# The first loads in another order, and six blocks of 384 tokens in place of nine of 256 ahead of the experts

## The chip, the cores and the metric

The kernel runs on one core of one Trainium2 chip. The metric is the device time of one execution in microseconds (us), the median of several runs. Times inside an execution come from a hardware trace of one profiled execution.

## The reference

The input is 2 sequences of 2048 tokens with 256 values each, 4096 tokens in all. A diagonal state layer with a residual is followed by a mixture of experts; each is followed by a layer norm.

```python
decays = sigmoid(x @ Wd + bd);  inj = x @ Wi + bi
h[t] = decays[t] * h[t-1] + inj[t]                  # a scan along the tokens
y = layernorm(x + layernorm(h) * gamma + beta + x)
gate = y @ Wg.T + routing_bias                      # 8 experts, the 4 best of each token
weights = softmax over the 4 best
ffn(u, w1, w2, w3) = (silu(u @ w1.T) * (u @ w2.T)) @ w3.T        # hidden size 682
out = layernorm(y + ffn(y, shared) + sum_e weights[e] * ffn(y, expert e))
```

## The kernel before

**First stage.** The tokens pass in eight steps (`NSTEP`) of 512, and the two sequences take turns. For step s, TensorE makes the products with Wd and Wi (`products`), ScalarE the decays and injections (`acts`), VectorE scans (`scan`), TensorE turns the states (`states`), VectorE takes the first norm and adds the residual u (`first_norm`), GpSimd works out the reciprocal deviations (`rstd1`, `rstd2`), ScalarE writes y (`normed`), TensorE turns y (`y_turned`) and makes the gate logits (`gates`). TensorE runs two steps ahead with the products.

**First loads.** SyncE issues, in this order: one half of the weights Wd and Wi (L479), the second half of the turned input of step 0, the other weights, the small parameters, the turned input of step 1, `load_residual(0)` (the rows of x for step 0, L485), `load_turned(2)` (the turned input of step 2, which waits for the products of step 0, because it goes to the same buffer), `load_residual(1)`. GpSimd adds half of beta to each residual (`add_beta`, L594) and fetches the shared weights into `stage` (`fetch(0)`, 2176 KB) between `add_beta(0)` and `add_beta(1)` (L624 to L626); its next work is `rstd1(0)`. ScalarE splits the staged weights in step order (`shared_high`), VectorE makes the low halves (`shared_low`).

**Blocks.** All feed-forward work goes in blocks of tokens against one weight set. Values and weights are held as two float16 parts, so a product is three matmuls. `up` makes six chunks of the hidden layer (66 matmuls as wide as the block), ScalarE takes the silu of each chunk, VectorE multiplies (`gated`), ScalarE rounds (`high`), VectorE makes the rest (`low`), and `down` takes the chunks back to 256 values. A block of `TB` = 256 tokens keeps a chunk in one bank of psA, so four chunks are in flight. A block of `TL` = 384 tokens needs two banks for a chunk, so two chunks are in flight (`chunk_bank`, L287), and its third group of down sums lies in bank 3 of psA, so that chunk 1 of the next block waits until these sums are read (`down_read`). An expert whose count of 128-row groups is odd ends on such a block.

**Order of blocks.** The shared expert runs over all 4096 tokens in 16 blocks of 256: `S1` = 9 ahead of the experts, seven behind them. Pieces of block 0's `up` fill TensorE's waits in steps 6 and 7 (`EARLY`). In the nine blocks, VectorE also does the routing: `chosen_early`, `chosen_late` (the four best of each token), `count`, `places` (the row in the experts' buffer for each token and choice), `weigh`, `pads`, `sizes`, and the low halves of y (`low_half`), and the low halves of expert 0's weights (`first_low`), of which ScalarE makes the high ones (`first_high`). VectorE runs strictly in the order of the code: one such step stands between two chunks' products, or between two blocks (L1520 to L1542).

**Rows for the experts.** When `places` and `weigh` are done, GpSimd scatters the rows of y to memory, 32 indirect DMAs for each of the four choices (`scatter_first` L675, then `scatter`), with expert weights converted beside them. SyncE loads the rows of an expert's blocks turned (L511) with their routing weights (L517) once the scatter for that choice has landed. At the end GpSimd gathers the experts' results back.

## Time and profile before

| | |
|---|---|
| median of 3 runs | 1010.56 us (1007.47 to 1012.38) |
| the profiled execution | 1012.52 us, of which the trace's span is 1010.8 us |
| TensorE (PE) busy | 982.8 us, 97% of the span |
| VectorE (DVE), ScalarE (ACT), GpSimd (POOL) busy | 56%, 51%, 54% |
| chain that ended last, by engine | PE 81%, DVE 6%, POOL 5%, issue 3%, ACT 2%, DMA 2% |

PE is TensorE's matmuls and PEld its weight loads; SPq, ACTq and POOLq are the queues' own instructions. L12 is line 12 of the kernel. In a timeline or a chain a row begins with its start and its length in us; what stands in square brackets is the idle time of the engine before it and what ended that. "x66" is the count of instructions merged into a row. Matmuls overlap, so a row's length is up to 0.17 us more than its share of time.

### The profile page before, as it was taken

The numbers are of one execution on the slowest core, as the hardware profiler recorded it, in microseconds if no ns is written. First come the engines' busy times: TensorE is split into PE (matmuls) and PEld (weight loads), VectorE is DVE, ScalarE is ACT, GpSimd is POOL, SyncE is SP. The second block draws the span as 40 slices with busy tenths as digits, with TensorE's granted clock in tenths as the row PEclk, the third lists the DMA queues.
The fourth block names the chain that finished last, engine by engine and source line by source line (L and its number), as shares of the span: only waits on it lengthen the run. The fifth ranks groups of instructions, "written<-read, shape, count | busy, mean of one in ns | idle before, by whom it ended". The sixth has DMA issues, their size and how long they took to land.

```text
span 1010.8 us, 25795 instructions
## 1 busy us (share of the span) xinstructions
PE 982.8 (97%) x8252; PEld 817.2 (81%) x8252; DVE 570.9 (56%) x1450; ACT 515.7 (51%) x1289; POOL 544.1 (54%) x513
## 2 busy tenths in 40 slices
PE   8999989999999999999999999999999999999987
PEld 3566878878887888888788878788888887887865
DVE  4899887756454555545445445445455454544776
ACT  3666634544454545545455445445455554544466
POOL 3554057669333377237471007066888880875882
PEclk9999999999999999999999999999999999999999
DMA  6766133453533333532514213317973882895694
GB/s 244 198 159 148 47 91 119 108 176 95 166 93 96 94 98 95 163 101 67 143 51 136 63 32 101 93 48 171 126 111 69 123 129 52 112 128 94 94 165 110
DMA packets 168052, 113.88 MB, mean 113 GB/s; under 512 B 113596, under 2 KB 160191, under 8 KB 166848
## 3 DMA queue, kind: packets, MB, share of 16 engines
q0 software_dynamic: 29808, 58.37, 27.1%
q1 hardware_dynamic: 115888, 33.15, 15.5%
q10 hardware_dynamic: 22304, 21.76, 6.5%
q8 instruction: 21, 0.34, 0.1%
q14 instruction: 31, 0.25, 0.1%
HBM read 47.09 MB, written 43.12 MB: 89 GB/s over the span
## 4 chain that ended last, share of the span: by engine, by line
PE 81%; DVE 6%; POOL 5%; issue 3%; ACT 2%; DMA 2%; SPq 1%; ACTq 0%; DVEq 0%; POOLq 0%
PE psA L1051 52%; PE psB L1082 20%; PE psA L999 4%; POOL y_sum L746 3%; PE psB L1085 2%; DVE g_lo L1476 1%; DMA work<-x_tok 1%; PE psC L1033 1%; PE psA L1082 1%; DVE psC L1466 1%; DVE g_hi L1476 1%; SPq L511 1%; ACT sil L861 1%; PE psC L1026 1%; DMA y_sum<-rows_by_place,place 0%
## 5 line engine op out<-in xcount | busy, mean ns | idle before, releaser
L861 ACT ACTIVATE sil<-psA 128x256 f32<-128x256 f32 (+1 forms) x474 | 181.8, 389 | 276.5 <-PE psA L1051 242.2
L746 POOL DMA_INDIRECT y_sum<-rows_by_place,place x128 | 200.5, 1566 | 80.8 <-issue 37.4
L1466 DVE SCALAR_TENSOR_TENSOR g<-psA,sil 128x256 f32<-128x256 f32 (+1 forms) x166 | 71.6, 432 | 298.3 <-ACT sil L861 298.1
L1051 PE MATMUL psA<-xb_odd,work 128*128 128x256 f16 x1980 | 221.1, 273 | 0.7 <-issue 0.4
L1051 PEld LDWEIGHTS psA<-xb_odd,work 128*128 128x128 f16 x1980 | 193.2, 98 | 24.5 <-issue 2.3
L1082 PE MATMUL psB<-work,g_hi 128*128 128x256 f16 x1260 | 211.4, 273 | 0.7 <-DVE g_lo L1476 0.4
L1051 PE MATMUL psA<-xb,work 128*128 128x256 f16 x1782 | 200.7, 274 | 2.6 <-issue 1.6
L1051 PEld LDWEIGHTS psA<-xb,work 128*128 128x128 f16 x1782 | 174.3, 98 | 25.9 <-issue 5.1
L1466 DVE SCALAR_TENSOR_TENSOR psC<-psA,sil 128x256 f32<-128x256 f32 (+3 forms) x308 | 136.1, 442 | 89.0 <-ACT sil L861 83.5
L1082 PE MATMUL psB<-work,g_lo 128*128 128x256 f16 x630 | 171.7, 273 | 0.0
L693 POOL DMA_INDIRECT rows_by_place<-y_rows,place x96 | 94.9, 988 | 133.7 <-DMA rows_by_place<-y_rows,place 119.1
L867 ACT ACTIVATE g_hi<-psC 128x256 f16<-128x256 f32 (+3 forms) x308 | 119.3, 387 | 43.5 <-DVE psC L1466 41.5
L1082 PEld LDWEIGHTS psB<-work,g_hi 128*128 128x128 f16 x1260 | 122.7, 98 | 17.1 <-DVE g_lo L1476 2.2
L1051 PE MATMUL psA<-xb,wshared 128*128 128x256 f16 x1056 | 119.0, 273 | 1.4 <-DVE g L1466 1.2
L1051 PEld LDWEIGHTS psA<-xb,wshared 128*128 128x128 f16 x1056 | 103.0, 98 | 14.0 <-DVE g L1466 1.5
L1476 DVE TENSOR_TENSOR g_lo<-psC,g_hi 128x256 f16<-128x256 f32 (+1 forms) x231 | 98.7, 427 | 2.4
L605 POOL TENSOR_SCALAR work<-stage 128x704 f16<-128x704 f32 (+1 forms) x42 | 35.0, 834 | 116.1 <-PE psA L1085 112.0
L1476 DVE TENSOR_TENSOR g_lo<-g,g_hi 128x256 f16<-128x256 f32 (+1 forms) x164 | 88.1, 537 | 4.7 <-ACT g_hi L867 1.1
L867 ACT ACTIVATE g_hi<-g 128x256 f16<-128x256 f32 (+1 forms) x166 | 69.6, 419 | 15.0 <-DVE g L1466 13.2
L1476 DVE TENSOR_TENSOR g_hi<-psC,g_hi 10x256 f16<-10x256 f32 (+3 forms) x154 | 65.8, 427 | 3.4
L1082 PEld LDWEIGHTS psB<-work,g_lo 128*128 128x128 f16 x630 | 61.6, 98 | 7.1
L1051 PE MATMUL psA<-xb_tail,work 128*128 128x384 f16 x396 | 65.8, 326 | 0.1
(167 smaller groups left out, 958.4 us busy)
## 6 DMA issues: line engine op xcount, KB each, us to landing
stage<-wpack POOLq DMA_DIRECT2D x9, 2176.0 KB, 9.3
rows_by_place<-eb ACTq DMA_DIRECT2D x57, 256.0 KB
work<-xT SPq DMA_DIRECT2D x7, 512.0 KB, 5.2
work<-half_beta SPq DMA_DIRECT2D x6, 512.0 KB, 4.4
work<-x_tok POOLq DMA_DIRECT2D x6, 512.0 KB, 6.1
rows_by_place<-eb ACTq DMA_DIRECT2D x6, 384.0 KB
rows_by_place<-zeros SPq DMA_DIRECT2D x1, 2112.0 KB, 12.1
rows_by_place<-y_rows,place POOLq DMA_INDIRECT x128, 2.5
```

The source lines that it names most:

```text
L511: sp.dma_start_transpose(out=xb[slot][:, :, j * P:(j + 1) * P], in_=xs_values[bass.ds(r0, P), :])\
L605: t.add(pool.tensor_scalar(parts_of(w, a, m)[0], stage[:, a:a + m], WS, 1.0, ALU.mult, ALU.mult))
L693: pool.indirect_dma_start(out=xs, out_offset=bass.IndirectOffsetOnAxis(ap=place[:, k, n:n + 1], axis=0), in_=y_rows[:, n, :], in_offset=No ...
L746: pool.indirect_dma_start(out=y_sum[:, n, :], out_offset=None, in_=xs, in_offset=bass.IndirectOffsetOnAxis(ap=place[:, k, n:n + 1], axis=0 ...
L861: act.activation(sil[r0:r0 + n, c % SLOTS, 0:T], psA[0:n, chunk_bank(c, T), 0:T], ACT.Silu, scale=1.0 / (XS * WS)).then_inc(silu_ready, 1)
L867: act.activation(g_hi[0:n, c, 0:T], gated_rows(g, c, 0, n, T), ACT.Copy).then_inc(gated_high_ready, 1)
L999: last = pe.matmul(psA[:, q, :], wdi[:, m, w, k, :], xt[b][:, k, :], start=(k == 0), stop=(k == KD - 1))
L1051: last = pe.matmul(dst, W[:, ws, k, ci, :], xb[slot][:, KD * xs_ + k, 0:T], start=(k == 0 and n == 0), stop=(k == KD - 1 and n == 2))
L1082: pe.matmul(o, a[:, c, j * P:(j + 1) * P], W3[:, ws, c, :], start=(c == 0 and n == 0), stop=False)
L1085: last = pe.matmul(o, g_hi[:, c, j * P:(j + 1) * P], W3[:, 1, c, :], start=False, stop=True)
L1466: dve.scalar_tensor_tensor(gated_rows(g, c, 0, n, T), src, 1.0 / (XS * WS), sil[r0:r0 + n, c % SLOTS, 0:T], ALU.mult, ALU.mult).then_inc(g ...
L1476: last = dve.tensor_tensor(dst, gated_rows(g, c, r, end, T), g_hi[r:end, c, 0:T], ALU.subtract)
```

## The change

The order of the first loads: SyncE issues `load_residual(1)` ahead of `load_turned(2)`. GpSimd's `add_beta(0)` waits for the first scan, `add_beta(1)` for the second, and `fetch(0)` stands behind both and waits until the turned input of step 2 has landed.

The blocks ahead of the experts: the same 2304 tokens go in `SA` = 6 blocks of 384. They use the two buffers of 384 rows that were the experts' last blocks' own. In steps 6 and 7 one chunk of block 0's `up` runs in each, a third behind the last `y_turned`, three behind the last `gates`. ScalarE takes two silus, not three, ahead of the last rows of y. The routing steps on VectorE are cut finer and have new places (`routed_beside`), and so have the halves of expert 0's weights. Block numbers behind the six move down by three. The seven shared blocks behind the experts, and the experts, are unchanged.

```diff
+    SA = S1 * JB // JL
+    assert SA * JL == S1 * JB
...
-        def step_of(i):
-
-            return B * (i % (NS // B) // JB) + i // (NS // B)
+        def step_of(n):
+
+            return B * (n % (NT // B) // JT) + n // (NT // B)
...
-            return (S1 - i) % 2
+            return 4 + (SA - i) % 2
...
+            def load_ahead(i):
+
+                sp.wait_ge(y_low_ready, max(low_rank(step_of(n)) for n in range(JL * i, JL * (i + 1))))
+                load_shared(i, JL * i, JL, early_slot(i))
...
             load_residual(0)
+            load_residual(1)
             load_turned(2)
-            load_residual(1)
...
-                    sp.wait_ge(y_low_ready, low_rank(step_of(0)))
-                    load_shared(0, 0, early_slot(0))
-
-            for i in range(1, S1):
-                sp.wait_ge(y_low_ready, low_rank(step_of(i)))
-                load_shared(i, i, early_slot(i))
+                    load_ahead(0)
+
+            for i in range(1, SA):
+                load_ahead(i)
...
+            pool.wait_ge(states_ready, 1)
             add_beta(0)
+            pool.wait_ge(states_ready, 2)
+            add_beta(1)
+            pool.wait_ge(xT_loaded[0], 32)
             fetch(0)
-            add_beta(1)
...
-                first = SLOTS if ahead else 1
+                first = 2 if ahead else 1
...
-            ffn_block(0, ahead=last_rows)
-            ffn_block(1)
+            ffn_block(0, TL, ahead=last_rows)
+            ffn_block(1, TL)
...
+                    if g == 2 and c == 1:
+                        first_high(0)
+                    elif g in (3, 4) and c in (1, 3):
+                        first_high(2 * g - 5 + c // 2)
+                    elif g == 5 and c == 1:
+                        first_high(5)
...
-                    up(SH, 0, [2 * (s - EARLY)], slot=early_slot(0))
+                    up(SH, 0, [s - EARLY], TL, early_slot(0))
...
-                if s >= EARLY:
-                    up(SH, 0, [2 * (s - EARLY) + 1], slot=early_slot(0))
             y_turned(NSTEP - 1)
-            up(SH, 0, [4, 5], slot=early_slot(0))
+            up(SH, 0, [2], TL, early_slot(0))
             gates(NSTEP - 1)
+            up(SH, 0, [3, 4, 5], TL, early_slot(0))
             pe.wait_ge(states_read, 2 * NSTEP)
-            down(SH, 0)
+            down(SH, 0, TL)
             pe.wait_ge(logits_ready, NSTEP)
-            ffn_block(SH, 1, slot=early_slot(1), between=ranks)
+            ffn_block(SH, 1, TL, early_slot(1), between=ranks)
...
+            def routed_beside(g):
+
+                def step(c):
+                    if g == 0 and c == 1:
+                        chosen_early()
+                    elif g == 1 and c == 1:
+                        shift()
+                    elif g == 1 and c in (2, 3):
+                        low_half(4, c - 2)
+                    elif g == 2 and c < 2:
+                        largest_keys(c * NT // 2, (c + 1) * NT // 2)
+                        if c == 1:
+                            places()
+                    elif g == 2 and c == 2:
+                        weigh()
+                    elif g == 2 and c == NC:
+                        first_low(0)
+                    elif g == 3 and c < 2:
+                        low_half(6, c)
+                    elif g == 3 and c < 4:
+                        low_half(1, c - 2)
+                    elif g == 3 and c == 4:
+                        block_counts()
+                    elif g == 3 and c == NC:
+                        low_half(3, 0)
+                        low_half(3, 1)
+                    elif g == 4 and c < 2:
+                        low_half(5, c)
+                    elif g == 4 and c < 4:
+                        low_half(7, c - 2)
+                    elif g == 4 and c == 4:
+                        block_words()
+                    elif g == 4 and c == NC:
+                        pads()
+                    elif g == 5 and c < 4:
+                        first_low(1 + c)
+                    elif g == 5 and c == NC:
+                        first_low(5)
+                return step
+
+            def ahead_tiles(g):
...
+            ffn_block(0, TL, beside=routed_beside(0))
...
-            add_shared(0, 0)
-            ffn_block(1, beside=shift)
+            add_shared(0, ahead_tiles(0))
+            ffn_block(1, TL, beside=routed_beside(1))
             count()
+            place_keys()
+            add_shared(1, ahead_tiles(1))
+            for g in range(2, SA):
+                ffn_block(g, TL, beside=routed_beside(g))
+                add_shared(g, ahead_tiles(g))
```

## Rows read from the trace of the kernel before

**Rows 1.** Windows by stage: us, busy time (instructions) of each engine, granted clock, DMA share, GB/s.

```profile
109.13:207.06 97.93, 92.52 (x820) 78.28 (x820) 76.01 (x266) 45.62 (x117) 52.45 (x53) 1.00 0.34 94
```

**Rows 2.** Timeline of all engines, first loads: start, length, engine, line, operation.

```profile
12.16 0.81 POOL L602 DMA_DIRECT2D stage<-wpack  x1
12.84 0.56 SPq L468 DMA_DIRECT2D work<-xT  x1
...
23.89 2.34 POOL L597 TENSOR_TENSOR work<-work,half_beta 128x1024 f32<-128x1024 f32 x1 [10.92 <-DMA work<-x_tok]
```

**Rows 3.** Timeline of PE in the first stage.

```profile
22.39 7.13 PE L999 MATMUL psA<-work,sm 128*128 128x512 f32 x16 [1.83 <-DMA work<-xT]
...
35.76 1.09 PE L1026 MATMUL psC<-ident,y_sum 128*128 128x128 f32 x8 [1.93 <-ACT y_sum L816]
36.69 5.29 PE L999 MATMUL psA<-work,sm 128*128 128x512 f32 x8
...
104.53 1.09 PE L1026 MATMUL psC<-ident,y_sum 128*128 128x128 f32 x8 [0.32 <-ACT y_sum L816]
```

**Rows 4.** Windows of 2 us with a granted clock of 0.50, columns as in rows 1.

```profile
38.00:40.00 2.00, 2.00 (x3) 0.66 (x2) 2.00 (x4) 0.86 (x1) 0.99 (x1) 0.50 1.09 341
...
208.00:210.00 2.00, 2.00 (x12) 1.36 (x10) 0.00 (x0) 0.35 (x1) 1.55 (x2) 0.50 1.10 331
```

**Rows 5.** DMA issues of the page: count, KB each, median us from issue to landing.

```profile
stage<-wpack POOLq DMA_DIRECT2D x9, 2176.0 KB, 9.3
...
work<-xT SPq DMA_DIRECT2D x7, 512.0 KB, 5.2
```

**Rows 6.** Chain that ended last: first expert block, then a 384-token block.

```profile
207.06 9.04 PE psA L1051 x66
...
317.60 10.73 PE psA L1051 x66
333.57 7.21 PE psA L1051 x66
```

**Rows 7.** Groups by shape, 222 to 920 us: chunk work of the 384-token blocks.

```profile
L861 ACT ACTIVATE sil<-psA 128x384 f32<-128x384 f32 x30 | 14.7, 490 | 35.0 <-PE psA L1051 34.1 <-DVE g L1466 0.9
...
L1466 DVE SCALAR_TENSOR_TENSOR psC<-psA,sil 128x384 f32<-128x384 f32 x18 | 10.2, 566 | 17.0 <-ACT sil L861 17.0
L1476 DVE TENSOR_TENSOR g_lo<-psC,g_hi 128x384 f16<-128x384 f32 x18 | 9.9, 551 | 0.2
```

**Rows 8.** Timeline of DVE: routing between the blocks.

```profile
111.35 0.19 DVE L1310 TENSOR_TENSOR gate_room<-psC,sm 128x32 f32<-128x32 f32 x1
...
115.96 0.75 DVE L1496 SCALAR_TENSOR_TENSOR y_sum<-psB,y_sum 128x256 f32<-128x256 f32 x2
...
122.73 0.42 DVE L1368 COPY work<-psC 128x256 f32<-128x256 f32 x1
...
127.49 2.27 DVE L1425 MAX8 top<-work 128x8 f32<-128x8 f32 x32
```

**Rows 9.** Groups of DVE, 84 to 225 us: the low halves of y.

```profile
L1289 DVE SCALAR_TENSOR_TENSOR y_rows<-y_sum,y_rows 128x512 f16<-128x512 f32 x12 | 8.2, 687 | 0.1
```

**Rows 10.** Timelines of POOL and SP: first scatter, loads of the first expert block.

```profile
133.36 1.13 POOL L682 DMA_INDIRECT rows_by_place<-y_rows,place  x1 [30.99 <-DVE y_rows L1360]
...
178.01 0.96 POOL L682 DMA_INDIRECT rows_by_place<-y_rows,place  x1 [0.30 <-issue]
...
190.94 3.30 SPq L511 DMA_TRANSPOSE xb<-rows_by_place  x2
195.35 0.43 SPq L517 DMA_DIRECT2D row_weights<-rows_by_place  x1
```

**Rows 11.** Timeline of POOL: expert 3's weights, converted behind the last scatter.

```profile
463.46 0.78 POOL L605 TENSOR_SCALAR work<-stage 128x704 f16<-128x704 f32 x1 [3.40 <-PE psB L1085]
...
485.06 0.60 POOL L602 DMA_DIRECT2D stage<-wpack  x1 [0.64 <-POOL work L620]
```

**Rows 12.** Chain that ended last: first block of expert 3.

```profile
513.08 7.21 PE psA L1051 x66
```

More of the change, by code:

```diff
@@ L763, in _ @@
                 if 1 <= e < E - 2:
-                    counted(pool, down_ready, done + S1)
+                    counted(pool, down_ready, done + SA)
                     convert(e + 3, e % 2)
@@ L919, in _, with first_high_beside @@
             act.wait_ge(table_loaded, 1)
-            for g in range(2, S1):
-                if g == 6:
-                    ffn_block(g, beside=lambda c: first_high(0) if c == 3 else None)
-                elif g == 7:
-                    ffn_block(g, beside=lambda c: first_high(1 + (c == 2)) if c in (0, 2) else None)
-                elif g == 8:
-                    ffn_block(g, beside=lambda c: first_high(3 + c // 2) if c in (0, 2, 4) else None)
-                else:
-                    ffn_block(g)
+            def first_high_beside(g):
+                def step(c):
[7 more added lines that the diff above has]
+            for g in range(2, SA):
+                ffn_block(g, TL, beside=first_high_beside(g))
             act.wait_ge(blocks_ready, 1)
@@ L965, in _ @@
                 lot = LOTS.index(i - 2) if i - 2 in LOTS else None
-                ffn_block(r + S1 + i, beside=None if lot is None else lambda c: norm_groups(lot, c, NC - 1))
+                ffn_block(r + SA + i, beside=None if lot is None else lambda c: norm_groups(lot, c, NC - 1))
                 if lot is not None:
@@ L1117, in read_first @@
                     nc.regs_alu(first, word, FIELD - 1, ALU.bitwise_and)
-                    nc.regs_alu(first, first, S1, ALU.add)
+                    nc.regs_alu(first, first, SA, ALU.add)
                 elif c == 2:
@@ L1198, in _ @@
             assert E // 2 <= NC
-            for g in range(2, S1):
-                ffn_block(SH, g, slot=early_slot(g), beside=read_sizes if g == S1 - 1 else None)
+            for g in range(2, SA):
+                ffn_block(SH, g, TL, early_slot(g), beside=read_sizes if g == SA - 1 else None)
             pe.wait_ge(first_low_ready, len(pieces) + len(MIXED))
@@ L1410, in sizes, with place_keys @@
                     .then_inc(blocks_ready, 1)
-            def places():
+            def place_keys():
                 t.add(dve.scalar_tensor_tensor(inc[:, :, :], start.unsqueeze(2).to_broadcast([P, E, NT]), -float(P),
@@ L1422, in places, with largest_keys @@
                 t.wait()
-                for n in range(NT):
+            def largest_keys(lo, hi):
+                for n in range(lo, hi):
                     ins = dve.max(top[:, n, :], key[:, n, :])
                 t.add(ins)
+            def places():
                 t.wait()
@@ L1480, in ffn_block @@
                     gated(c)
-                    if c == at and beside:
-                        beside()
-                    if rows_at and c in rows_at:
-                        low_half(*rows_at[c])
-                    if first_lows and c in first_lows:
-                        first_low(first_lows[c])
+                    if beside:
+                        beside(c)
                     if c:
@@ L1489, in ffn_block, with add_shared @@
                 low(NC - 1)
-            def add_shared(g, i):
+                if beside:
+                    beside(NC)
+            def add_shared(g, tiles):
                 dve.wait_ge(down_ready, g + 1)
-                for j in range(JB):
-                    n = i * JB + j
-                    ins = dve.scalar_tensor_tensor(one(y, n), psB[:, j, 0:D], 1.0 / WS, one(y, n), ALU.mult, ALU.add)
+                for j, n in enumerate(tiles):
+                    ins = dve.scalar_tensor_tensor(one(y, n), down_sum(j), 1.0 / WS, one(y, n), ALU.mult, ALU.add)
                 ins.then_inc(down_read, 1)
@@ L1514, in _, with step @@
             t = early
-            def beside_first():
-                chosen_early()
-            ffn_block(0, beside=beside_first)
+            def routed_beside(g):
+                def step(c):
+                    if g == 0 and c == 1:
[33 more added lines that the diff above has]
+                        first_low(5)
+                return step
+            def ahead_tiles(g):
+                return range(JL * g, JL * (g + 1))
+            ffn_block(0, TL, beside=routed_beside(0))
             logits(NSTEP - 1)
@@ L1606, in moments_beside @@
                         t.add(ins)
-                ffn_block(g, beside=moments_beside if lot else None)
+                ffn_block(g, beside=(lambda c: moments_beside() if c == 1 else None) if lot else None)
                 if lot and LOTS.index(i - 1) != POOL_LOT:
@@ L1612, in _ @@
                 gathered(ORDER.index(S1 + i))
-                add_shared(g, S1 + i)
+                add_shared(g, range(JB * (S1 + i), JB * (S1 + i + 1)))
             counted(dve, down_read, g + 2)
```

62 lines of the change are left out of this document (24 added, 38 removed).

## The prediction, made before the changed kernel ran

> **What bounds the kernel now.** I read the table of the page first: TensorE is busy for 97% of the span, and the chain that ended last lies on it. So a time is gained only where TensorE waits or runs slowly, and the next view is its timeline with the idle times. There are two such places ahead of the experts. In the first stage it waits 1.83 us for the turned input of step 2 and 1.93 us for the first rows of y, and the eight products after that take 5.29 us, where sixteen take 7.13 [rows 3]; in that stretch the granted clock is 0.50, the 1.2 GHz level, in place of 1.00 [rows 4]. The second place is the stretch from the shared blocks' first `down` to the first expert block: 97.9 us with 92.5 busy [rows 1], and the expert block that follows spends 9.04 us on an `up` that costs 7.21 elsewhere [rows 6], again with the clock at 0.50 [rows 4] after waits. VectorE is busy for 76 of these 97.9 us [rows 1], the only engine beside TensorE that is near its limit there. Behind that, the work follows the experts' blocks and shifts as a whole.
>
> **Part 1, the first loads.** What is late today: the turned input of step 2 is issued at 12.84, just behind GpSimd's fetch of 2176 KB at 12.16 [rows 2], and is used at 22.39 [rows 3], 9.5 us after its issue; the median of such a load is 5.2 us [rows 5]. The rows of x for step 1 stand behind it on SyncE's queue. GpSimd waits for them 10.92 us, to 23.89, and adds beta for 2.34 us [rows 2], to 26.23; only then comes the first reciprocal deviation, and 9.5 us later, at 35.76, y is turned [rows 3].
>
> What moves: `load_residual(1)` goes ahead of `load_turned(2)`, so it is issued when SyncE has nothing else to wait for, some 9 us earlier. `fetch(0)` goes behind the turned input. That input, issued at 12.84 with nothing beside it, lands at 12.84 + 5.2 = 18.0. TensorE is ready for it at 22.39 - 1.83 = 20.56, so the wait of 1.83 us goes. On GpSimd the two additions wait for the two scans (an estimate of 11.5 and 14.9, because the second scan follows products that today end near 13), so they end near 14.9 + 2.34 = 17.2, the fetch is issued at 18.0 to 18.9, and `rstd1(0)` is free 7 us earlier than today. What is late next is VectorE, which needs the turned states of step 0 for its moments; TensorE turns those 3.57 us (half of 7.13) ahead of 20.56, and I allow 2.5 us for scan and moments: 19.5. Then y would be ready at 19.5 + 9.5 = 29.0. TensorE comes to it at 20.56 + 6.96 (sixteen products) + 0.93 (eight turns, as 35.76 to 36.69) + 3.57 = 32.0. So the wait of 1.93 us goes too, with 3 us to spare. Without these waits I count the clock as staying up: 5.29 - 3.57 = 1.72 us. The moved instructions cost SyncE nothing (it waits for products), and the fetch lands at 18.9 + 9.3 [rows 5] = 28.2, about when ScalarE first wants it (20.56 + 6.96 + one activation, 28.2), so nothing is lost but nothing is spare.
>
> Sum of part 1: 1.83 + 1.93 + 1.72 = **5.5 us**, from 0 (the waits come back elsewhere) to 6. From there to step 6 TensorE has no idle row, so the shift holds.
>
> **Part 2, width alone.** A block of 384 costs 10.73 us of `up` and is followed 15.97 us later by the next one [rows 6], so `down` is 5.24. Three blocks of 256 (7.21 + 5.24 x 2/3 = 10.70 each) are 32.1, two of 384 are 31.9. Six for nine give 0.5 us. The width is worth little in itself; what counts is the waits.
>
> **Part 3, the shared blocks' waits.** I set the new order against today's times, from the last `y_turned` at 104.53 [rows 3], which ScalarE's rows of y set; the pieces of `up` ahead of it fit into TensorE's waits, as now. The turns take 0.93, gates for eight pairs some 1.7 (16 small matmuls, by TensorE's time up to today's first `down`), and the left chunks of block 0 (one is 10.73 x 12/66 = 1.95, the last half of that) 6.83: `down` of block 0 starts at 114.0 and ends at 119.2. Five blocks of 15.97 and the ranks (0.2) would end at 199.3. The waits:
> - VectorE finishes a block 3.2 us behind the end of `up`: silu 0.49, gated 0.57, high and its copy about 1.0, two low parts 0.55 each [rows 7]. For block 0 that is 117.2. The last logits and `chosen_late` take 115.96 - 111.35 = 4.6, and the three additions 0.75 x 3/2 = 1.1 [rows 8], to 122.9. Chunk 1 of block 1 needs the down sums read and could go at 121.2: 1.8 us of wait, new with this change, because a 256 block has no such wait before its chunk 3.
> - After block 1, `count` and the keys (122.73 to 127.49 without the additions between them: 4.1) now both stand ahead of the additions [rows 8]: VectorE is free at 135.0, done at 140.2, TensorE could go at 139.1: 1.1 us.
> - In block 2 the maxima of the keys (2.27, in two halves) and `weigh` (four passes like the 0.42 at 122.73) [rows 8] push one product back: I work out 0.9 us.
> - Blocks 3 to 5: a chunk with a low half of y costs VectorE 0.57 + 0.69 + 0.55 = 1.81 [rows 7, 9] against TensorE's 1.95, so it is covered. In `down` there are 5.24 us for VectorE's 3.2; today there are 3.5, so each step put late into a 256 block shows as a wait.
>
> Waits of 3.8 us in all: the first expert block can start at 203.2 + 0.6 (today's gap of the loop) = 203.8, in place of 207.06 [rows 6]. That gives 3.3 us, and as no wait stands shortly before it, 9.04 - 7.21 = 1.8 of clock [rows 6]. Sum: **5.1 us**. The unknown is what the clock does after the new wait of 1.8 us: today it fell behind waits of 1.93 and stayed up behind others; a fall costs 1.7 to 1.8 [rows 3, 6]. I take none, and one for the range.
>
> **What stands behind it.** The scatter starts when `weigh` is done: today at 133.36 [rows 10]; by the walk above at 148.9, 15.5 later. It takes 44.7 us to its last issue [rows 10], 193.6; a landing is somewhere between nothing and the 5.2 of a 512 KB load [rows 5], I take 2.5. Turning two groups takes 3.3, the routing weights an issue of 0.43 [rows 10] and a small load, about 1.5: 201.3, against 203.2 for TensorE. Covered by 1.9 us. Further on, expert 3's weights are converted from 463.46, after 3.40 us of waiting for TensorE, to 485.06 [rows 11], and wanted at 513.08 [rows 12]. With the scatter 15.5 later GpSimd starts them at 460.06 + 15.5 = 475.6 and ends at 497; they are wanted at 508. Covered by 11 us.
>
> **Sum.** 5.5 + 5.1 = 10.6 us off the profiled execution's 1012.5 gives 1001.9. The median of the runs shown is 2.0 lower than that execution, so on it 1010.56 - 10.6 = **1000.0 us**.
>
> **The rivals.**
> 1. *The fetch collides with the next input.* `load_turned(3)` is issued when step 1's products are done, at 20.56, now beside the fetch of 18.9. If it takes 9.5 us, as step 2's did, it lands at 30.1; TensorE wants it at 20.56 + 6.96 + 0.93 = 28.5. It loses 1.6 and the clock's 1.72: 1003.3 us. Against it: the fetch has a start of 1.7 us here and no third load in between. The Trainium skill's page "DMA: Bandwidth & Descriptors", section "Issuing engines are not separate DMA queues", says that loads from different engines run on the same sixteen DMA engines and interleave. By that rule moving the fetch only chooses whom it delays, and the 9.5 us beside the fetch agree with it.
> 2. *The scatter sets the experts' start.* If the last landing takes 5.2, and the routing weights as long, the first block is ready at 201.3 + 2.7 + 3.7 = 207.7, 4.5 behind TensorE, and the clock falls in that wait: 6.3 us, 1006.3 us. For it: the margin is 1.9 us. Against: today's issues are a steady 1.3 us or so apart.
> 3. *Two chunks in flight are too few (slower).* Chunk c + 2 waits for the product of chunk c. If a low half of y and a low part stand in the queue ahead of each product, the answer takes 0.49 + 0.69 + 0.55 + 0.57 + 0.1 = 2.4 us and TensorE has 1.95: 0.45 us for each of 30 chunks is 13.5, and one fall of the clock on the way 1.8: 1015.3 us, up to 1022 with one in each block. It decides as soon as a chunk's work on VectorE is over 1.95 us. Against it: the sum is 1.81, and in the experts' 384 blocks the next block came with no wait [rows 6]. The Trainium skill's page "Perfetto Trace Analysis", section "Optimization Strategy", says that a gap that repeats can mean too little PSUM for the next tile; rows 6 do not show it for such blocks, but there VectorE had no routing work.
> 4. *Part 1 does not do what it says.* The additions beside a scan, or VectorE, hold up the first y as long as today: 1000.0 + 5.5 = 1005.5 us.
>
> **How the numbers follow.** Forecast 0.64, with a range of its own from 996.5 (no new waits, 3.8 less, within the spread of the runs) to 1004 (two falls of the clock); rival 1 0.13, rival 2 0.10, rival 3 0.08, rival 4 0.05. About 0.5%, 5 us, is what a measurement can tell from no change here. Below 1005.5 lie nearly all of the forecast (0.63) and of rival 1 (0.12), and some of rivals 2 and 4 (0.04): 0.79. Slower than 1015.6 is the larger part of rival 3 and what I have not seen: 0.06. The rest, 0.15, is within 0.5%. The range of 996 to 1006 leaves out rival 3 and the outer half of rival 2.
>
> **What would show it.** In the changed profile: no idle row on TensorE ahead of the products of step 2 and of the first turned y, and no clock of 0.50 near 37 us; y turned first at about 32. One wait of about 1.8 us in chunk 1 of block 1 and one of about 1 in block 2; none in blocks 3 to 5. The first expert block at 207.06 - 5.5 - 3.3 = 198.3, with an `up` of 7.2. The prediction is wrong if SyncE's first expert load comes after TensorE is done with the sixth block, if the clock falls more than twice, or if blocks 3 to 5 follow each other in more than 16.0 us.

## The result, and the profile after

| | median of the executions, us | lowest to highest | ratio to the kernel before, 95% interval |
|---|---|---|---|
| before (18 executions) | 1008.11 | 1003.28 to 1015.91 | |
| after (18 executions) | 1003.41 | 1000.98 to 1007.12 | 0.9949 (0.9930 to 0.9969) |
| before, the profiled execution | 1012.52, span 1010.8 | | |
| after, the profiled execution | 1002.12, span 1000.3 | | |

The change gains 0.5%: the ratio is worth 5.1 us (3.1 to 7.1), and the two medians differ by 4.7. The forecast was a gain of 10.6 us and a median of 1000.0, 3.4 below the measured one. The two profiled executions differ by 10.4 us; the medians differ by half of that. Both numbers are right, and the experiments are about the difference: the kernel before has executions that are over 12 us apart, and its profile shows one near their long end.

TensorE's timeline of the kernel after, in order: the last products of step 1 with those of step 2, the first products of step 3, the first turned y, the waits in the shared blocks, the last three shared blocks, the first expert block (start us, us, engine, line, operation; in brackets the idle time before it and what ended it).

```profile
16.69 10.46 PE L1011 MATMUL psA<-work,sm 128*128 128x512 f32 x24
27.87 3.60 PE L1011 MATMUL psA<-work,sm 128*128 128x512 f32 x8
31.30 1.04 PE L1038 MATMUL psC<-ident,y_sum 128*128 128x128 f32 x8
...
116.79 8.94 PE L1063 MATMUL psA<-xb_tail,wshared 128*128 128x384 f16 x54 [1.67 <-DVE y_sum L1512]
134.08 7.96 PE L1063 MATMUL psA<-xb_tail,wshared 128*128 128x384 f16 x48 [0.94 <-DVE y_sum L1512]
142.34 1.15 PE L1063 MATMUL psA<-xb_tail,wshared 128*128 128x384 f16 x6 [0.30 <-DVE g L1485]
148.56 10.89 PE L1063 MATMUL psA<-xb_tail,wshared 128*128 128x384 f16 x66
164.53 10.89 PE L1063 MATMUL psA<-xb_tail,wshared 128*128 128x384 f16 x66
180.49 10.89 PE L1063 MATMUL psA<-xb_tail,wshared 128*128 128x384 f16 x66
...
198.36 7.38 PE L1063 MATMUL psA<-xb,work 128*128 128x256 f16 x66 [1.74 <-DMA row_weights<-rows_by_place]
```

The two waits of the first stage are gone [rows 3]: the 24 products are one row without a gap, and y is turned at 31.30 in place of 35.76. The waits in the shared blocks are where the walk put them. What it did not have is the last bracket: TensorE was ready at 196.62 and waited 1.74 us for the routing weights of the first rows. The next rows show why, with GpSimd's first and last scatter for the first choice, the landing, SyncE's turned loads (two), its load of the weights, and that landing.

```profile
142.35 1.13 POOL L690 DMA_INDIRECT rows_by_place<-y_rows,place  x1 [46.19 <-DVE y_rows L1371]
187.72 1.62 POOL L690 DMA_INDIRECT rows_by_place<-y_rows,place  x1 [0.30 <-issue]
...
187.72 3.10 DMA rows_by_place<-y_rows,place
192.22 3.15 SPq L516 DMA_TRANSPOSE xb<-rows_by_place  x2
196.33 0.43 SPq L522 DMA_DIRECT2D row_weights<-rows_by_place  x1
196.33 1.89 DMA row_weights<-rows_by_place
```

The last scatter has landed at 190.82; SyncE's first load is 1.40 us later, and between its second load (ended 195.37) and the weights lie 0.96 us more.

### The profile page after: what moved, and what is told of

It is laid out like the page before. It is cut to its first block, busy times and chain, and to the rows that moved or that the text cites. A ratio compares the mean times of both kernels' runs of the same rounds, so it can differ in the third digit from the quotient of the medians.

```text
span 1000.3 us, 25270 instructions
## 1 busy us (share of the span) xinstructions
PE 975.2 (97%) x8054; PEld 798.4 (80%) x8054; DVE 562.6 (56%) x1411; ACT 509.3 (51%) x1250; POOL 545.3 (55%) x513
## 4 chain that ended last, share of the span: by engine, by line
PE 79%; POOL 6%; DVE 6%; issue 3%; DMA 3%; ACT 1%; SPq 1%; ACTq 0%; DVEq 0%; POOLq 0%
PE psA L1063 49%; PE psB L1094 19%; PE psA L1011 5%; POOL y_sum L754 3%; POOL rows_by_place L690 2%; DMA rows_by_place<-y_rows,place 2%; PE psB L1097 2%; DVE g_lo L1495 1%; PE psC L1045 1%; PE psA L1094 1%; SPq L516 1%; DVE g_hi L1495 1%; DVE psC L1485 1%; PE psB L1024 1%; DMA y_sum<-rows_by_place,place 1%
## 5 line engine op out<-in xcount | busy, mean ns | idle before, releaser
L869 ACT ACTIVATE sil<-psA 128x256 f32<-128x256 f32 (+1 forms) x456 | 178.8, 399 | 287.3 <-PE psA L1063 266.9
L1485 DVE SCALAR_TENSOR_TENSOR psC<-psA,sil 128x256 f32<-128x256 f32 (+3 forms) x296 | 133.1, 449 | 82.7 <-ACT sil L869 77.8
L875 ACT ACTIVATE g_hi<-psC 128x256 f16<-128x256 f32 (+3 forms) x296 | 116.5, 394 | 37.0 <-DVE psC L1485 34.9
L1495 DVE TENSOR_TENSOR g_lo<-psC,g_hi 128x256 f16<-128x256 f32 (+1 forms) x222 | 96.6, 435 | 2.3
L1495 DVE TENSOR_TENSOR g_lo<-g,g_hi 128x256 f16<-128x256 f32 (+1 forms) x158 | 85.3, 540 | 4.6 <-ACT g_hi L875 0.4
L610 POOL TENSOR_SCALAR work<-stage 128x704 f16<-128x704 f32 (+1 forms) x42 | 35.7, 849 | 94.1 <-PE psA L1097 93.4
L1063 PE MATMUL psA<-xb_tail,wshared 128*128 128x384 f16 x396 | 66.3, 326 | 2.9 <-DVE y_sum L1512 2.6
L617 POOL TENSOR_TENSOR work<-stage,work 128x704 f16<-128x704 f32 (+2 forms) x42 | 63.4, 1509 | 2.9
```

Of the source, the lines that this page charges most:

```text
L610: t.add(pool.tensor_scalar(parts_of(w, a, m)[0], stage[:, a:a + m], WS, 1.0, ALU.mult, ALU.mult))
L617: t.add(pool.tensor_tensor(lo[:, 0:full], stage[:, a:a + full], hi[:, 0:full], ALU.subtract))
L869: act.activation(sil[r0:r0 + n, c % SLOTS, 0:T], psA[0:n, chunk_bank(c, T), 0:T], ACT.Silu, scale=1.0 / (XS * WS)).then_inc(silu_ready, 1)
L875: act.activation(g_hi[0:n, c, 0:T], gated_rows(g, c, 0, n, T), ACT.Copy).then_inc(gated_high_ready, 1)
L1063: last = pe.matmul(dst, W[:, ws, k, ci, :], xb[slot][:, KD * xs_ + k, 0:T], start=(k == 0 and n == 0), stop=(k == KD - 1 and n == 2))
L1485: dve.scalar_tensor_tensor(gated_rows(g, c, 0, n, T), src, 1.0 / (XS * WS), sil[r0:r0 + n, c % SLOTS, 0:T], ALU.mult, ALU.mult).then_inc(g ...
```

## Experiments

### 1. Each half alone, and both kernels again

`loads_only` is the kernel before with the first loads as in the change, `blocks_only` the kernel after with the loads as before, `before_again` and `after_again` are the two kernels unchanged. The four ran on one chip, beside 35 executions of before with a median of 1007.69.

```
 # loads_only, SyncE                # loads_only, GpSimd
+load_residual(1)                   +pool.wait_ge(states_ready, 1)
 load_turned(2)                      add_beta(0)
-load_residual(1)                   -fetch(0)
                                    +pool.wait_ge(states_ready, 2)
                                     add_beta(1)
                                    +pool.wait_ge(xT_loaded[0], 32)
                                    +fetch(0)
```

> The kernel before with the new order of the first loads alone; the shared blocks stay nine of 256 rows. The prediction's own terms: 5.5 us shorter than before (1.83 for the turned input of step 2, 1.93 for the first y, 1.72 for the clock), the first y turned at about 32, and the first expert block about 5.5 us earlier than 207.06. Rival, the clock falls only in some executions: 3.8 us by the median, and up to 5.5 beside an execution with the fall. Rival, the first loads of before land earlier in most executions than in the profiled one: 0 to 2 us by the median, although the profile shows the first y at 32.

> The kernel after with the old order of the first loads; the shared blocks are six of 384 rows. The prediction's own terms: 5.1 us shorter than before (3.3 at the first expert block and 1.8 for the clock behind it), that block at about 203.8 with a first group of about 7.2. Rival, scattered rows set the experts' start as the profile of after has it (1.74 waited for the row weights): 5.1 less about 1.7, so some 3.4, with the same wait ahead of the first expert block. Rival, the clock does not fall at the experts' start of before in most executions: 1.5 to 3.3 us.

> The kernel before, unchanged, to see which of its waits are the same in a second profiled execution. If the front's waits and the two falls of the clock belong to the kernel, this profile has again 1.8 to 1.9 us ahead of the products of step 2 and of the first y, the clock at 0.50 near 38 and near 208, and a time within 2 us of 1012.5. If they belong to the one execution, at least one of them is gone and the time is 1004 to 1008. The ratio to the kernel before is 1.000 within 0.3 per cent either way.

> The kernel after, unchanged, beside the two halves of the change on the same chip. If the halves add, its gain is the sum of theirs within 1.5 us: 10.6 us by the prediction, 5 us by the medians so far. If a part takes from the other (both end at the same wait for the row weights), the sum of the halves is larger than its gain by that wait, about 1.7 us. Its profile should have the wait for the row weights ahead of the first expert block again, between 1 and 2.5 us, and no clock of 0.50 before it.

| kernel | median of 12 | ratio to before, 95% interval | y first turned | first expert block | last expert rows stored | experts' phase |
|---|---|---|---|---|---|---|
| before (profiled execution above) | | | 35.76 | 207.06 | 924.74 | 717.7 |
| before_again | 1006.14 | 0.9993 (0.9963 to 1.0023) | 31.44 | 201.13 | 916.66 | 715.5 |
| loads_only | 1004.55 | 0.9975 (0.9950 to 0.9999) | 31.44 | 201.03 | 914.29 | 713.3 |
| blocks_only | 1006.35 | 0.9978 (0.9953 to 1.0003) | 35.59 | 202.31 | 917.72 | 715.4 |
| after (profiled execution above) | | | 31.30 | 198.36 | 913.48 | 715.1 |
| after_again | 1002.85 | 0.9963 (0.9938 to 0.9989) | 31.98 | 199.25 | 913.00 | 713.8 |

The four columns on the right are of one execution each: the start of a row of TensorE, the start of ScalarE's last store of expert rows, and the difference of the last two.

The ratios give 2.5 us for the loads (0.1 to 5.0) and 2.2 for the blocks (0.3 longer to 4.7 shorter), against 3.7 for both (1.1 to 6.2). So the halves add within this noise, and no finer statement can be made; the interval of `blocks_only` alone does not tell it from before. Its profile has the wait for the row weights that the scatter's rival named (1.26 us, 1.93 in `after_again`); its 2.2 us lies in the range of the rival of the clock, too. `after_again` was expected to have no window at 0.50 ahead of the experts, and has one at 90 to 92 us.

The line of `before_again` is the finding. The same kernel, not a letter changed, turns its first y at 31.44, as the change does, and has no wait there. The first rows are TensorE's first turned y and first expert block and GpSimd's, VectorE's and SyncE's first stage in this execution. The second are VectorE's first scan and the addition beside it in the execution of rows 2 and 3, which the prediction did not read:

```profile
9.87 1.28 DVE L1240 TENSOR_TENSOR_SCAN work<-work,start_state 128x512 f32<-128x512 f32 x1 [8.31 <-ACT work L807]
10.04 3.25 POOL L597 TENSOR_TENSOR work<-work,half_beta 128x1024 f32<-128x1024 f32 x1 [2.63 <-DMA work<-x_tok]
12.47 0.56 SPq L468 DMA_DIRECT2D work<-xT  x1
13.25 0.81 POOL L602 DMA_DIRECT2D stage<-wpack  x1
31.44 1.09 PE L1026 MATMUL psC<-ident,y_sum 128*128 128x128 f32 x8
201.13 7.38 PE L1051 MATMUL psA<-xb,work 128*128 128x256 f16 x66 [0.62 <-issue]
```

```profile
9.87 2.35 POOL L597 TENSOR_TENSOR work<-work,half_beta 128x1024 f32<-128x1024 f32 x1 [2.46 <-DMA work<-x_tok]
10.24 3.06 DVE L1240 TENSOR_TENSOR_SCAN work<-work,start_state 128x512 f32<-128x512 f32 x1 [8.69 <-ACT work L807]
```

In the first, the scan begins first and the addition takes 3.25 us; the fetch goes out at 13.25, behind the turned input of 12.47. In the second, the addition begins first, takes 2.35, and it is the scan that takes 3.06 in place of 1.28; the fetch goes out at 12.16, ahead of the input of 12.84 [rows 2]. Some tenths of a microsecond at 10 us settle which transfer stands behind which, and with it 6 us: the first expert block is at 201.13 in the one and at 207.06 in the other. In the second, TensorE's clock fell near 38, on the way there, and once more near 208, behind that block's start [rows 4]; in the first it fell at neither place. The other profiles with the old order of the loads go the same way. In `add_first` (experiment 2) and `blocks_only` the addition begins ahead of the scan, the fetch ahead of the input, and y comes at 35.6; in `scan_first` and `fetch_first` all three are the other way round, and y comes at 31.3 to 31.5.

### 2. The order forced

`scan_first`: GpSimd's first addition waits for VectorE's first scan; nothing else is changed in the kernel before. `add_first` is its mirror. `fetch_first` lets SyncE issue the turned input only after GpSimd's fetch.

```
 # scan_first, GpSimd               # add_first, VectorE, in scan(s, m)
+pool.wait_ge(states_ready, 1)      +if (s, m) == (0, 0):
 add_beta(0)                        +    dve.wait_ge(residual_ready, 1)

 # fetch_first, GpSimd              # fetch_first, SyncE
 fetch(0)                           +sp.wait_ge(fetch_issued, 1)
+pool.sem_inc(fetch_issued, 1)       load_turned(2)
```

> The kernel before with one wait added: GpSimd adds beta for step 0 only when VectorE has done the first scan, so the fetch goes out some 1.5 us later, at about 13.8, and behind the turned input. The loads keep their old order. Theory of the two orders: y first turned near 31.5 in the profile, as in the loads' new order, and a median of 1003.5 to 1005.5, the same as the new order of the loads alone gave (1004.55). Rival (it is the order of SyncE's two loads that counts, not the fetch): the first y waits for the residual behind the input and the fetch, y first turned at 33 to 36, and the median stays at 1007 to 1008.

> The kernel before with one wait added, the mirror of the scan-first kernel: VectorE does the first scan only when GpSimd has added beta for step 0, so the fetch goes out at about 12.2, ahead of the turned input, in every execution. Theory of the two orders: y first turned near 35.7, the last y turned at 102.7 to 104.5 and the first expert block at 205 to 207 in the profile, and a median of 1009.5 to 1012, above that of before on the same chip by 1 to 3 us and above the scan-first kernel by 4 to 6. Rival (the front's waits are given back further on): the median stays within 0.5 us of before and below 1009.

> The kernel before with one wait added: SyncE issues the turned input of step 2 only when GpSimd has issued its fetch, so the order of the profiled execution of before is forced in every execution. Theory of the two orders (an execution of before has the front's waits or has not, by whether the fetch or the input goes out first): y first turned near 35.7, the last y turned near 104.5 or 102.8, the first expert block 6 us later than in an execution with the input first, and a median of 1009 to 1012, 2 to 4 us above that of before. Rival (what differs between executions is the clock and the end, not the front): y first turned near 35.7 in this profile too, but the median stays within 1 us of before.

| kernel | median of 12 | lowest to highest | before on that chip | ratio, 95% interval | first expert block |
|---|---|---|---|---|---|
| scan_first | 1005.43 | 1002.34 to 1008.14 | 1009.51 | 0.9962 (0.9942 to 0.9981) | 200.97 |
| add_first | 1010.57 | 1007.32 to 1014.08 | 1008.14 | 1.0017 (0.9992 to 1.0042) | 207.06 |
| fetch_first | 1011.38 | 1002.27 to 1014.72 | 1009.51 | 1.0014 (0.9995 to 1.0032) | 200.79 |

One wait of GpSimd gains 3.8 us (1.9 to 5.9), beside 2.5 for the whole new order of the loads; the intervals overlap. The mirror kernel gives the profile of before again, with its falls of the clock; GpSimd, SyncE and TensorE of `add_first`, and one window:

```profile
12.11 0.81 POOL L602 DMA_DIRECT2D stage<-wpack  x1
12.82 0.56 SPq L468 DMA_DIRECT2D work<-xT  x1
22.25 7.13 PE L999 MATMUL psA<-work,sm 128*128 128x512 f32 x16 [1.72 <-DMA work<-xT]
35.61 1.09 PE L1026 MATMUL psC<-ident,y_sum 128*128 128x128 f32 x8 [1.92 <-ACT y_sum L816]
207.06 9.04 PE L1051 MATMUL psA<-xb,work 128*128 128x256 f16 x66 [0.61 <-issue]
...
208.00:210.00 2.00, 2.00 (x11) 1.38 (x10) 0.00 (x0) 0.31 (x1) 0.26 (x1) 0.50 0.96 400
```

The two forced kernels differ by 1.0017 / 0.9962 = 1.0055, 5.6 us (2.3 to 8.8, an estimate from the two intervals). They ran on two chips, each beside the kernel before, whose median lies above `scan_first` on the one and below `add_first` on the other. Together with the profiles that carries the theory of the two orders. The interval of `add_first` alone does not tell it from before. Both kernels set the order of scan and addition; the order of the two loads followed from it and was not forced by itself.

`fetch_first` did not force what it was meant to: in its profile the input goes out at 12.34 and the fetch at 13.07. GpSimd's increment stands behind the fetch in its program, but it had come before the fetch's row began. The profiled execution is the fastest of its twelve (1002.27); the other eleven lie from 1006.78 up, and no profile shows their order. So its expectation, y near 35.7, missed (31.26); it is one more execution with the input first, and no test of the order.

### 3. What is late at the experts' start

`sums_first` (in the kernel after) reads the down sums of blocks 0 and 1 ahead of routing steps; `scatter_early` makes the inputs of the scatter earlier; `both_early` has the edits of both. Of the edits the main lines are shown.

```
 # sums_first, VectorE                     # scatter_early
 largest(EARLY_TILES, NT)                  # ScalarE: exponentials ahead of ffn_block(1)
-choose(EARLY_CHOSEN, NT)                  # VectorE:
+choose(20, 25)                            largest(EARLY_TILES, NT)
+add_shared(0, ahead_tiles(0))            +shift()
+choose(25, NT)                            # block 1, chunk 1:
 # block 0, chunk 2:                      -shift()
+choose(EARLY_CHOSEN, 20)                 +weigh()
 # ahead of block 1:                       # block 2, chunk 0:
-add_shared(0, ahead_tiles(0))            -largest_keys(0, NT // 2)
 # behind block 1:                        +largest_keys(0, NT)
 count()                                  +places()
+add_shared(1, ahead_tiles(1))             # block 2, chunks 1 and 2:
 place_keys()                             -largest_keys(NT // 2, NT)
-add_shared(1, ahead_tiles(1))            -places()
                                          -weigh()
```

> The kernel after with VectorE's routing steps in another order: the down sums of block 0 are read in the middle of the choice of experts (of whose tiles 12 are chosen earlier, in block 0) and those of block 1 ahead of the keys. It takes away TensorE's waits of 1.67 in block 1 and 0.94 in block 2; what the scatter needs is as late as before or only 1 us earlier. Theory (the scatter sets the experts' start): those two waits are gone, the wait for the row weights ahead of the first expert block grows from 1.7 or 1.9 to 3.5 to 4.5, the first expert block stays between 197.4 and 199.3, and the time stays that of after within 1 us. Rival (TensorE's own waits set it): the first expert block 2.6 us earlier, at about 196, and the time 2.6 us shorter.

> The kernel after with the scatter's inputs made earlier and TensorE's waits left: the exponentials run on ScalarE ahead of block 1, the routing weights are made in block 1 and the places in one piece at the start of block 2. The first scatter is issued some 3 to 4 us earlier than 142.35. Theory (the scatter sets the experts' start): the wait for the row weights of 1.7 to 1.9 is gone, the first expert block is at about 197 with today's gap of 0.6, and the time 1.5 us shorter than that of after; the shift adds 0.4 to the wait in block 1, so 1.1 to 1.7. Rival (something behind the scatter, such as SyncE's loads of rows, has a time of its own): the first expert block stays at 198.4 to 199.3.

> The two edits together: the down sums ahead of the routing steps, and the scatter's inputs earlier. Theory: each of them alone leaves the other's lateness; together the first expert block comes at 194.5 to 196 in place of 198.4 to 199.3, and the time is 3 to 4.5 us shorter than that of after, 998 to 1000. Rival (the gain is given back further on, because GpSimd's conversions or the end of the kernel do not move with it): the first expert block at 195, but the time within 1.5 us of that of after.

| kernel | median (executions) | ratio to before, 95% interval | first scatter | wait ahead of the first expert block | first expert block | experts' phase |
|---|---|---|---|---|---|---|
| after | 1003.41 (18) | 0.9949 (0.9930 to 0.9969) | 142.35 | 1.74 | 198.36 | 715.1 |
| sums_first | 1000.01 (6) | 0.9932 (0.9905 to 0.9959) | 140.16 | 1.66 | 196.10 | 716.8 |
| scatter_early | 1002.68 (12) | 0.9953 (0.9924 to 0.9981) | 139.56 | 0.38 | 198.29 | 715.9 |
| both_early | 999.30 (9) | 0.9923 (0.9897 to 0.9948) | 136.13 | 0.28 | 194.22 | 716.8 |

The three ran beside a kernel before of 1007.09. The first expert blocks of sums_first, scatter_early, both_early, and the row of scatter_early that answers to 116.79 above:

```profile
196.10 7.38 PE L1063 MATMUL psA<-xb,work 128*128 128x256 f16 x66 [1.66 <-DMA row_weights<-rows_by_place]
```

```profile
116.83 10.64 PE L1063 MATMUL psA<-xb_tail,wshared 128*128 128x384 f16 x54 [2.00 <-DVE y_sum L1514]
198.29 7.38 PE L1063 MATMUL psA<-xb,work 128*128 128x256 f16 x66 [0.38 <-issue]
```

```profile
194.22 7.38 PE L1063 MATMUL psA<-xb,work 128*128 128x256 f16 x66 [0.28 <-SPq L519]
```

The expectation for `sums_first` missed: it said that the wait would grow and the block stay. The wait stayed, since the scatter came forward with TensorE, and the block came 2.3 us earlier than in after. `weigh` stands behind chunk 2 of block 2, so each wait of TensorE ahead of that chunk delays the scatter too. Two things that were weighed as alternatives, TensorE's waits and the scatter, are in series up to block 2 and parallel only from there. `scatter_early` took the wait for the weights away, as expected (0.38 is left), but in this execution the clock fell behind the wait of 2.00: 10.64 us for what takes 8.94 above, 1.70 us. Without it the block would be at 196.6, an estimate. Why its ratio to before (0.9953) is no lower than that of after (0.9949) was not settled. Together the edits bring the block to 194.22, 4.1 us ahead of after, and the shortest time of a kernel that computes all: 999.3. The intervals of all three ratios overlap that of after, so a gain over after is read from the profiles and not shown by the times.

### 4. What else differs between executions

With the front and the clock put aside, the experts' phase still takes from 713.0 (`fetch_first`) to 718.1 us (`scan_first`). Neither has a window with the clock at 0.50 in it. The difference sits in single blocks, such as this one of `scan_first`; VectorE, GpSimd and TensorE:

```profile
364.64 0.42 DVE L1477 TENSOR_TENSOR g_lo<-psC,g_hi 128x256 f16<-128x256 f32 x1
365.96 2.17 DVE L1477 TENSOR_TENSOR g_lo<-g,g_hi 128x256 f16<-128x256 f32 x1
366.31 1.53 POOL L612 TENSOR_TENSOR work<-stage,work 128x704 f16<-128x704 f32 x1
368.19 0.39 PE L1083 MATMUL psB<-work,g_hi 128*128 128x256 f16 x2 [0.47 <-DVE g_lo L1477]
```

The low part of chunk 3 takes 2.17 us in place of 0.42, ends just behind GpSimd's subtraction of an expert's weights, and TensorE's `down` waits for it. `low_off` is the kernel after without that subtraction: it leaves out the low parts of the experts' weights.

```
-t.add(pool.tensor_tensor(lo[:, 0:full], stage[:, a:a + full], hi[:, 0:full], ALU.subtract))
+t.add(pool.memset(lo[:, 0:full], 0.0))
```

> The kernel after with GpSimd's subtraction for the low parts of the experts' weights replaced by writing zeros, which reads nothing: that part of the computation is left out. Theory (VectorE's low part of a product that lies in SBUF waits for a GpSimd subtraction that began first, and these collisions spread the experts' phase): the rows of such low parts over 1.2 us (four to nine of them in the profiles so far, up to 2.5) are gone or under 1.0, the time from the first expert block to the last scaled rows falls from 713.0 to 718.1 to 711 to 713, and the executions lie within 3 us of each other but for the clock; median 999.5 to 1002. Rival (the long rows are covered by TensorE and the spread comes from the clock or the DMA): the long rows are gone, but the phase still takes 713 to 715 and the spread of 5 to 6 us stays.

Measured: median 998.77 us (six executions, 997.37 to 1001.05), ratio 0.9906 (0.9872 to 0.9939) beside a before of 1008.14. The first expert block is where it was in after (198.29, behind 1.88 us for the weights), and the phase takes 712.0 us in place of 715.1. All low parts of the experts' blocks of 256 tokens from 203 to 905 us, in groups (line, engine, operation, shapes, count, then busy us, mean ns, idle before), first of after, then of low_off:

```profile
L1495 DVE TENSOR_TENSOR g_lo<-psC,g_hi 128x256 f16<-128x256 f32 x171 | 71.3, 417 | 1.8
L1495 DVE TENSOR_TENSOR g_lo<-g,g_hi 128x256 f16<-128x256 f32 x113 | 62.6, 554 | 4.0
```

```profile
L1495 DVE TENSOR_TENSOR g_lo<-psC,g_hi 128x256 f16<-128x256 f32 x171 | 71.4, 418 | 1.8
L1495 DVE TENSOR_TENSOR g_lo<-g,g_hi 128x256 f16<-128x256 f32 x113 | 52.3, 463 | 4.3
```

The same instruction reads its product from psC in three of five full chunks and from `g` in the other two. Only the second form is ever long: its mean is 554 ns, beside 417 for the first form in the same execution, and 463 without GpSimd's subtraction. One long row is left in `low_off` (1.76 us at 248.67, beside GpSimd's rounding and rescaling of a stage). The phase is 3.1 us shorter than in after and 1.8 shorter than in `after_again`. Five of six executions lie within 2.2 us (997.37 to 999.52), but the sixth makes the spread 3.7, and the expected median of 999.5 to 1002 was missed on the low side. The write of zeros is also shorter than the subtraction (0.70 us in place of 1.53), so GpSimd's later work moves too; that was not separated.

The length of the low parts alone does not make the spread. `fetch_first`, with the short phase, has a mean of 558 ns and rows as long as this one (VectorE, GpSimd):

```profile
236.78 2.45 DVE L1479 TENSOR_TENSOR g_lo<-g,g_hi 128x256 f16<-128x256 f32 x1
237.28 1.66 POOL L614 TENSOR_TENSOR work<-stage,work 128x768 f16<-128x768 f32 x1
```

It is the low part of chunk 0 and ends at 239.23, before TensorE is through with the block's `up` (240.33). The next block's `up` starts 10.86 us after this one's, against 10.70 in `low_off`. In `scan_first` the block with the 2.17 us in chunk 3 takes 12.18. So it goes in the twelve profiles with the subtraction. Beside the same block of `low_off` (where that one has no long row itself), 32 blocks with a low part of chunk 3 over 1.3 us take 0.4 to 1.6 us more; 14 with one of chunk 0, and chunk 3's at 1.0 or less, take 0.0 to 0.3 more. Of the first kind `scan_first` has six and `fetch_first` none. So what a collision costs depends on the chunk that it falls on, and nothing in the program sets that.

## Why the prediction was right and wrong

**What bounds it, and where the work can be gained.** Right. The spans of the two profiles differ by 10.5 us; 8.7 of it lie ahead of the first expert block (207.06 to 198.36) and 1.7 in that block's slow `up` (9.04 to 7.38).

**Part 1, the first loads (5.5 us).** Right in each size for the execution it was read from. The waits of 1.83 and 1.93 and the slow products went [rows 3]; y came at 31.30 (32.0 forecast), the fetch at 17.22 (18.0 to 18.9), TensorE's 24 products without a gap. From profile to profile the last turned y moved from 104.53 to 98.31, 6.2 us in place of 5.5. The step that failed is one that the text takes without a word, that rows 2 and 3 are how the kernel before runs. They are one of two ways, and `before_again` and `scan_first` show the other. The margin between the two was in the rows that were quoted: 12.16 against 12.84 [rows 2], and the scan of 3.06 us was not read. The share of executions with the fetch first is only an estimate: 2.5 of 5.6 us, 0.45, from `loads_only`, and 3.8 of 5.6, 0.7, from `scan_first`. So part 1 is worth 2.5 to 4 us in place of 5.5, an estimate with the width of those intervals.

The Trainium skill's page "SBUF — State Buffer", section "Who interferes with whom", has a rule that fits this: a VectorE instruction with two inputs in SBUF and a GpSimd instruction that reads SBUF contend for a pair of ports that is an exclusive lock, and the order of issue decides which of them is held up. The rows agree: 3.25 and 1.28 us in one order, 2.35 and 3.06 in the other, and 417 against 554 ns in experiment 4 for products in PSUM and in SBUF. The order of issue itself is not seen there: the long row at 365.96 starts ahead of GpSimd's at 366.31.

**The clock (1.72 and 1.8 us).** The size is right (1.70 in `scatter_early`), but the falls do not come in every execution. Near 38 it fell in `before` and `add_first`, and not in `blocks_only`, which waited 1.16 and 1.92 us there. With nine blocks the window near 208 fell to 0.50 in `before` and `add_first`, both with the fetch first, and stayed at 1.00 in `before_again`, `loads_only`, `scan_first` and `fetch_first`, behind the same waits of 1.12 and 0.6 us. So 3.5 of the 10.6 us belonged to executions like the profiled one. Why the clock falls behind a wait at one time and not at another stays open.

**Part 2, the width (0.5 us).** Blocks 3 to 5 start 15.97 and 15.96 us apart and are as long as taken; the 0.5 us by itself was not measured.

**Part 3, the waits.** Forecast 1.8, 1.1 and 0.9, measured 1.67, 0.94 and 0.30; no waits in blocks 3 to 5. TensorE was ready for the first expert block at 196.62. The walk gave 203.2 in the time of before, and 197.0 with the 6.2 us taken off. Rival 3, too few chunks in flight, has no row.

**What stands behind it (a margin of 1.9 us).** This is the term that was wrong in size, and it changed the sign: the wait was 1.74 (rival 2, in small). Forecast in the time of before: last issue 193.6, landing 196.1, rows ready 201.3; less 6.2 that is 187.4, 189.9 and 195.1. Measured: 187.72, 190.82 and 198.22. The start of the scatter and its length were right. The 3.1 us are 0.6 more for the landing, SyncE's 1.40 from the landing to its first load, 0.96 from its second load to that of the weights, and 0.3 of the last issue; small rest. The second gap could be read: rows 10 have 4.41 us from SyncE's first load to its load of the weights, where the sum took 3.3. The sign that the prediction set (SyncE's first expert load behind TensorE's sixth block) did not show it: that load is at 192.22, 4.4 us ahead, and the rows were still 1.6 us late. So part 3 is not worth 3.3 + 1.8 between executions with the input first. From the last turned y to the first expert block it is 102.4 to 102.6 us with nine blocks (`before_again`, `loads_only`, `scan_first`, `fetch_first`) and 100.1 and 100.3 with six (`after`, `after_again`): 2.1 to 2.6 us.

**Sum.** 2.5 to 4 us of part 1 and 2.1 to 2.6 of part 3 make 4.6 to 6.6; measured were 5.1 (3.1 to 7.1). The forecast took 10.6 us off a median of three executions, 1010.56; over 18 it is 1008.11. So the gain was put 5.5 us too high and the level 2.4, and the second error took away part of the first. From the right level the same sum gives 997.5, 5.9 below the measured 1003.41; that this lies inside 996 to 1006 is in part luck.

Rival 1 (the fetch collides with the input of step 3) did not come: step 3's products begin at 27.87 with no wait, and so does y at 31.30. Rival 4 did not come in the profile either.

## What to carry to other kernels

Ahead of a sum on one profile, look at the spread of the times: 1003 to 1016 us for one kernel said that something in it has two outcomes, and the profile stood at one end. Look in it for two events within a microsecond whose order matters and that no wait sets, and put the wait there: one wait on GpSimd gained 3.8 us, the new order of three loads 2.5, with intervals that overlap. When two engines get in each other's way, look at which of the held-up steps another engine waits for: the same long row cost 0.0 to 0.3 us in one chunk and 0.4 to 1.6 in another. When two chains meet at one point, write both out to the last gap, the quiet engine's own steps too, and see from which point they are separate at all.

## What the hardware showed

- VectorE and GpSimd get in each other's way by where the inputs lie: 417 ns for a product in PSUM, 507 to 586 in the executions with GpSimd's subtractions for one in SBUF, single rows up to 2.48.
- VectorE's long row can begin ahead of the GpSimd row that it waits for (365.96 and 366.31); that the ends match, not the starts, shows who had to wait.
- An increment behind a DMA in GpSimd's program is no sign that the DMA was issued: in `fetch_first` SyncE went on at 12.34, and the fetch's row starts at 13.07.
- A fall of the clock ahead of another wait can cost nothing: in `after_again` it fell at 88 to 92 us, ahead of a y that was late anyway, and the next turned y came 7.10 us behind it, as in after (7.09).
